# Expert stage of an attention and mixture-of-experts kernel: where TensorE transposes the gated values

## The reference, cut to what matters

```python
x = x + xattn(layernorm(x), ctx)          # two softmax attentions, 8 heads of 64, 32 batches of 256 tokens
# then a mixture of 16 experts, 4 per token, on h = layernorm(x), 8192 tokens of 256 values:
probs = softmax(h @ gate_w.T);  topk_w, topk_idx = top_k(probs, 4);  topk_w /= sum(topk_w)
g = h @ w1[e];  u = h @ w3[e]             # 256 -> 128, for each chosen expert e
act = silu(g) * u                         # silu(g) = 0.5 g (1 + tanh(g/2))
out = sum over chosen e of topk_w[e] * (act @ w2[e])     # 128 -> 256
x = x + out
```

## Time and profile before

| What | us |
|---|---|
| Median of 3 runs | 2147.49 |
| Lowest and highest | 2143.29, 2151.18 |
| The profiled execution, own time | 2151.62 |
| Its span in the trace | 2149.9 |
| PE busy over the span | 1904.3 (89%) |
| Expert stage, first gate and up product to the last gated transposes | 1507.6 to 2017.5 |

### The profile page before, as it was taken

One profiled execution on the slowest core, in us unless ns is written; L12 is line 12 of the kernel. 1 busy time (PEld: TensorE's weight loads), 2 busy tenths in 40 slices (PEclk: granted clock), 3 DMA queues, 4 the chain that ended last, 5 costly groups with the idle time before them and its releaser, 6 DMA issues.

```text
span 2149.9 us, 51903 instructions
## 1 busy us (share of the span) xinstructions
PE 1904.3 (89%) x15782; PEld 1662.2 (77%) x15783; DVE 1388.3 (65%) x3231; ACT 1233.6 (57%) x3605; POOL 1222.7 (57%) x1688
## 2 busy tenths in 40 slices
PE   6899999999999999999999999997888988888400
PEld 5788888888888888888888888885788887888400
DVE  4567666666666766667776677768655545554398
ACT  5666666667666666666666666664444444444300
POOL 3356666656666666666666666666455555555400
PEclk9999999999999999999999999998999999999755
DMA  4331111111111111111111111117475444544399
GB/s 130 111 103 45 42 49 49 52 44 39 48 46 59 44 39 42 44 52 34 39 37 44 52 34 39 37 40 214 151 222 163 147 149 147 149 146 148 117 411 361
DMA packets 158561, 210.80 MB, mean 98 GB/s; under 512 B 24224, under 2 KB 131376, under 8 KB 158512
## 3 DMA queue, kind: packets, MB, share of 16 engines
q1 hardware_dynamic: 123696, 129.95, 19.8%
q0 software_dynamic: 26112, 71.86, 9.3%
q10 hardware_dynamic: 8704, 8.39, 1.1%
HBM read 113.02 MB, written 97.12 MB: 98 GB/s over the span
## 4 chain that ended last, share of the span: by engine, by line
PE 65%; DVE 9%; issue 7%; POOL 7%; DMA 5%; ACT 4%; another core or an unknown queue 2%; SPq 0%; ACTq 0%; POOLq 0%; DVEq 0%
PE p_pt L1366 10%; PE p_gu L1570 9%; PE p_s L1349 8%; PE p_av L1386 8%; PE p_s L1287 7%; PE p_x L1287 4%; DVE z_ahead L1254 4%; POOL x_rows L575 3%; PE p_y L1591 3%; POOL probs L583 3%; PE p_x L1417 3%; PE p_s L1297 3%; DMA x_rows<-routed,slot_i 2%; ACT probs L708 2%
## 5 line engine op out<-in xcount | busy, mean ns | idle before, releaser
L583 POOL TENSOR_TENSOR probs<-probs,inv 128x256 f32<-128x256 f32 x1024 | 596.9, 613 | 410.2 <-DVE inv L971 408.9
L708 ACT ACTIVATE probs<-p_s,nmx 128x256 f32<-128x256 f32 x1024 | 473.6, 481 | 74.4 <-PE p_pt L1366 43.4
L964 DVE TENSOR_REDUCE nmx<-p_s 128x4 f32<-128x1024 f32 x256 | 312.2, 1220 | 120.2 <-PE p_s L1349 120.2
L575 POOL DMA_INDIRECT x_rows<-routed,slot_i x248 | 247.4, 998 | 134.8 <-DVE target L956 70.5
L1366 PE MATMUL p_pt<-ident,probs 128*128 128x128 f32 x2048 | 292.8, 279 | 6.8 <-POOL probs L583 4.5
L1386 PE MATMUL p_av<-probsT,val 128*64 128x256 f32 x2048 | 259.2, 389 | 9.9 <-DVE probsT L859 7.0
L1366 PEld LDWEIGHTS p_pt<-ident,probs 128*128 128x128 f32 x2048 | 230.6, 142 | 40.1 <-issue 11.7
L696 ACT COPY probsT<-p_pt 128x512 f32<-128x512 f32 x256 | 151.3, 591 | 169.1 <-PE p_pt L1366 168.3
L859 DVE COPY probsT<-p_pt 128x512 f32<-128x512 f32 x256 | 176.0, 687 | 70.6 <-PE p_pt L1366 35.7
L708 ACT ACTIVATION_READ_ACCUMULATOR probs<-p_s,nmx 128x1 f32 x1024 | 216.4, 211 | 0.0
L1211 DVE TENSOR_TENSOR xgT_lo<-p_xt,xgT_hi 128x512 fp32r<-128x512 f32 x144 | 99.1, 688 | 176.8 <-ACT xgT_hi L816 151.0
(11 more groups left out here) (234 smaller groups left out, 5206.9 us busy)
## 6 DMA issues: line engine op xcount, KB each, us to landing
y_in<-y_rows SPq DMA_DIRECT2D x32, 1024.0 KB, 8.3
xg<-x_rows SPq DMA_DIRECT2D x72, 257.0 KB
xg_more<-x_rows SPq DMA_DIRECT2D x72, 257.0 KB
rows<-in_ctx_dram SPq DMA_DIRECT2D x32, 256.0 KB, 2.7
x_in<-in_x_dram SPq DMA_DIRECT2D x32, 256.0 KB, 2.9
mid_rows<-x_mid SPq DMA_DIRECT2D x32, 256.0 KB
x_rows<-bias SPq DMA_DIRECT2D x32, 256.0 KB, 3.4
z_ahead<-mid_rows SPq DMA_DIRECT2D x24, 256.0 KB
```

The lines of the kernel that those rows point to most:

```text
L575: pool.indirect_dma_start(x_rows, bass.IndirectOffsetOnAxis(ap=slot_i[:, t, k:k + 1], axis=0), to_send[:, t, k, :], None).then_inc(last_se ...
L583: pool.tensor_tensor(pr[:, h, t, :], pr[:, h, t, :], rc[:, g:g + 1].to_broadcast([P, S]), ALU.mult).then_inc(normed_p, 1)
L708: act.activation(probs[u % 2][:, h, t, :], p_s[:, 2 * (u % 2) + h, t * S:(t + 1) * S], ACT.Exp, bias=nmx[u % 2][:, g:g + 1], accum_out=sum ...
L964: dve.tensor_reduce(nmx[i][:, :], p_s[:, 2 * i:2 * i + 2, :].rearrange("p h (t k) -> p (h t) k", t=ST), AX.X, ALU.max, negate=True).then_i ...
```

## The change

Within PE's step the gated transposes of group j-2 move from behind the gate and up products of group j to ahead of them. Their waits, semaphores and the table's transposes move with them. Nothing is added or removed, and no other engine's code changes.

```diff
                             mm = pe.transpose(p_xt[:, i, n, k, :], xg[(r + 2) % LOADS][:, n, k * P:(k + 1) * P], ident[:, :])
                     mm.then_inc(xg_t, 1)
+                if exists(j - 2):
+                    pe.wait_ge(act_set, j - 1)
+                    wait(pe, actT_lo, j - 3)
+                    if isinstance(j, int) and j in (TABLE_AT, TABLE_AT + 1):
+                        v = j - TABLE_AT
+                        pe.wait_ge(plan_step, PLAN)
+                        for c in range(TC):
+                            pe.transpose(p_at[0:1, i, (2 + c) * P:(3 + c) * P], table[:, v, c:c + 1], ident[:, :])
+                    for n in range(2):
+                        mm = pe.transpose(p_at[:, i, n * P:(n + 1) * P], gated[i][:, n, :], ident[:, :])
+                    mm.then_inc(act_t, 1)
                 if exists(j):
                     experts[r] = expert_of(j)
                     pe.wait_ge(xgT_lo, j + 1)
...
                     mm.then_inc(gu_done, 1)
-                if exists(j - 2):
-                    pe.wait_ge(act_set, j - 1)
-                    wait(pe, actT_lo, j - 3)
-                    if isinstance(j, int) and j in (TABLE_AT, TABLE_AT + 1):
...
-                    for n in range(2):
-                        mm = pe.transpose(p_at[:, i, n * P:(n + 1) * P], gated[i][:, n, :], ident[:, :])
-                    mm.then_inc(act_t, 1)
                 if exists(j - 4):
```

## The result

| What | us |
|---|---|
| Changed kernel, median of 16 runs (lowest, highest) | 2156.45 (2151.03, 2161.28) |
| Kernel before, beside it, median of 16 runs (lowest, highest) | 2146.83 (2143.29, 2151.41) |
| Ratio, 95% interval | 1.0041, 1.0034 to 1.0049 |
| The profiled execution of the changed kernel, own time, span | 2156.23, 2154.5 |

The change costs 9 us: it lies in the range and within 0.5%, but by another mechanism than the likeliest one. It was the rival "the runs get shorter". That the time still fell close to the forecast of 2150 is in part luck: the price of a shorter run happens to be small. All ratios in this document leave out one slow run, the one of `p7_after` (the last of the experiments) at 2797.94 us with a mean granted clock of 0.678 (0.96 in the others; the median in its row counts it).

What follows compares the result with a forecast made beforehand. Bound: POOL's runs of scatters and their releases, not PE's work. Steady part 0, start +1, end +1 gave +2 us: 2153.6 for the profiled execution, 2149.5 as median, say 2150; range 2134 to 2182.

Steps and rivals of the forecast that it cites:

- the runs get shorter: Rival: the fifth scatter misses its run, runs hold four, 1.805 us a scatter; +13 us, 2160; chance 0.14.
- The bound: Expert stage: POOL's runs of scatters and each release, when ACT sees PE's posts late, set the pace, not PE's work.
- Work 0: PE's step: the same two gated transposes, 0.22 us, are made elsewhere, so PE's sum changes by 0.
- The wait at the release of the down products: Gate and up products now wait for actT_lo there: start some 1.15 us late, step ends 0.9 us late.
- The wait at the other release: Where DVE's gated step releases the products: 0.55 to 0.7 us late, 0.22 of it coming back.
- The slow stretch says that 0.8 us is absorbed: Stretch from 1663.95 at low PE clock took 8.91 us against 8.93, so PE's lateness costs 0 in the steady part.
- the first rival: Rival that PE's lateness is not absorbed, a release slipping if the fifth scatter waits for y_out; +28 us, chance 0.19.
- Not absorbed: Rival: PE's lateness after the release of the down products makes releases slip; +28 us, 2176; chance 0.19.
- the circle gets faster: Rival: act_t comes 1.4 us earlier, saving ACT's tanh waits, or runs of six form; -13 us, 2136; chance 0.20.
- The start: Step 5 now waits for the plan before its products, up to 2.0 us late; taken as +1 us.
- The end: Step 142: products wait for actT_lo and start 2.6 us late; between 0 and +2.6, taken as +1 us.
- The clock: Rival: longer waits lower PE's clock twice a cycle and PE becomes the bound; +20 us, 2170; chance 0.04.

Runs made afterwards that it cites:

- p7_after: The changed kernel with POOL's second scatter of a group waiting for xgT_hi of six groups on instead of seven; 2040.71 us, 1.0012 to the kernel before.
- e1_again: The changed kernel with the expert's number read ahead of the gated transposes' waits, on a chip with late releases; 2151.23 us, 1.0016 to the kernel before.
- after_again: The changed kernel unchanged, measured once more beside the kernel before on a chip with late releases; 2157.00 us, ratio 1.0043.
- p7_before: The kernel before with POOL's second scatter waiting for xgT_hi of six groups on, not seven; 2037.19 us, ratio 1.0002.
- e4: The kernel before with 8 of the 12 gate and up matmuls, third pass left out; 1996.04 us, ratio 0.9810.

## Why the prediction was right and wrong, step by step

**The bound, right.** Not PE's work but the runs of scatters set the pace in the result: PE was busy 12 us less after and the stage still took longer. The distances of a run's parts hold too: 2.13 us from its last scatter to ACT (2.26 said) and 1.34 us to the next run.

**Work 0, right.** PE's busy time did not grow.

**The wait at the release of the down products, mis-sized.** Said: transposes 0.25 us behind actT_lo, products 1.15 us late. Measured: actT_lo ended 1661.87, transposes at 1662.02, products 1.99 us after the release against 1602.1 - 1600.79 = 1.31 said, so 1.8 late. The missing 0.6 to 0.7 is the expert's number. I had priced it at the other release only; it stands behind the transposes' wait at both. The down products behind them ended 2.75 us into the run at 1662.66, where 1.8 to 2.0 was said, and this post is the one that was held in 20 of the runs of four.

**The wait at the other release, mis-sized.** Said 0.55 to 0.7 us late, with the number's 0.6 us beginning as soon as the wait ends. Measured: the transposes start 1.23 us into the run (1.34 said, right), and the number is begun at 1823.6, after them. It takes 0.8 us to its check, with a load of 519 ns where the earlier trace rows has 298, and 0.25 to the products. They start 2.45 us into the run, against 1594.48 - 1593.47 = 1.01 before: 1.44 late, twice what was said.

**"The slow stretch says that 0.8 us is absorbed", the step that failed.** Its lateness was real and did cost nothing: the products of that run ended 1667.45, 3.50 us in, against 2.69 in the run at 1593.47 (the prediction gives the 0.8 without these rows), and the cast behind them still started at once.

```profile
1667.04 0.41 PE L1570 MATMUL p_gu<-wgu_hi,xgT_lo 128*128 x1
1667.55 0.59 ACT L816 CAST xgT_hi<-p_xt 128x512 fp32r<-128x512 f32 x1 [1.77 <-issue]
```

I read from it a room in time and carried it to another order of posts. In that run, as in the one at 1593.47, the products' post was the second in its run. In the changed kernel the gated transposes' post stands ahead of it by the change itself, and the down products' post often as well. And it was a room for one post, the gate and up products'; for the down products nothing had been measured. The change also used more than the room: 1.44 us late where up to 0.7 was said, and 1.8 where 1.15 was said. So two things failed, the sizes and the use of the room. The runs that tell them apart are e1_again's: their gate and up products are 0.46 us late (1813.18 is 1.47 into the run), less than the 0.8 that was absorbed, and still it has 25 runs of four.

**The rival "the runs get shorter", right in kind, too dear.** It said 7.22 / 4 = 1.805 us a scatter and +13. The runs of four come at 7.16, 1.789 a scatter, and ten runs of five remain; the steady part measures +6 by the scatters from 1550 to 2010 us, and the total +9. The trigger that I named under the first rival, y_out of the fifth scatter, ended 20 of the 52 runs of four; xgT_hi of seven groups on, which I had not weighed, ended 32. "2.0 is before 3.2", which spoke against it, did not hold: the down products ended 2.75 us in, and were held all the same.

**"Not absorbed" (+28), wrong.** The releases don't slip one by one; a missed fifth scatter moves into the next run, which is a loss of 0.02 us a scatter and not of 1 us a run.

**The rival "the circle gets faster", wrong.** ACT's tanh no longer waits for the transposes' post, and no time came back, so that wait was not on the path. Only one run of six stands in the changed kernel's timeline.

**The start, right in place and unresolved in price.** The plan's last step ended 1525.19 and the products of group 5 started 1526.21, 1.02 us behind it; 0.74 or 1.14 was said (the terms named, 0.25 + 0.44 + 0.6, add up to 1.29; the 1528.3 is 0.15 too early by them). Before, they started 0.86 us ahead of its end. **The end, likewise**: in step 142 actT_lo ended at 2015.00 and the products started at 2016.03, 1.03 behind; 0.45 was said. What of this reached the end is in no trace alone. On the chips without late releases the whole change costs about 2 us by p7_after, both ends included.

**The clock, wrong.** The granted clock from 1550 to 2010 us was 1.00 (2.4 GHz) in the changed kernel (0.99 in after_again) and 0.98 before, with the transposes together and more waiting. The rule of the Trainium skill (TensorE: Matmul & The Clock Gate, Part 4: PE-mode transpose), by which it should come down more often, did not show.

**What stays open.** Of the 0.43%, the number's place explains 0.27%. The other 0.16% is the wait for actT_lo, the transposes' post ahead of the products', or both; the kernels that would divide it met chips where there is nothing to divide. Which of PE's posts are held in a run is open: their place among the others orders the gate and up products and fails for the down products. Why one chip has late releases and others don't, nothing here says.

## What to carry to other kernels

When two engines are coupled by a semaphore that arrives late, ask for each post that a move delays when it now falls, who needs it, and what is read or loaded behind the moved wait; a margin in microseconds taken from one post in the old order does not carry over to another post or another order. If PE's waits are moved ahead of its large products, move the register loads ahead of the waits with them: that alone gave back 0.27% of 0.43% here. Find out what a wait is for from the code's counts and not only from the row's name: the row of the scatter at 1670.10 names a cast that it does not wait for. And compare a small change on more than one chip before calling it a property of the kernel: here the change costs 0.4% on one and about 0.1% on another.

## What the runs showed of the hardware that was not expected

- The same kernel takes 2147 us in the result and in one further set on one chip, and 2035 to 2038 us on three other chips. That the chip is the cause is not shown. The products of the expert stage take 505.0 us from first to last in the one trace (1507.6 to 2012.6) and 403.3 in that of p7_before (1500.0 to 1903.3), 102 of the 113 us between the spans. With late releases, some semaphores that PE posts during a run of scatters are seen by ACT only about 2.0 to 2.3 us after the run's last scatter has started; on the other chips POOL scatters up to 238 times in 300 us (e4), and in the trace of p7_before, from 1550 to 1850 us, ACT goes on within 0.37 us of the post in all of its 107 waits over 0.1 us.
- With late releases, gate and up products whose post is the first or second of PE in a run are seen in 0.04 to 0.92 us (kernel before), the fourth or fifth after 3.1 to 5.4. Down products that are the second post were held too (after the change: median 3.05 us).
- Reading the expert's number takes PE's sequencer 0.6 to 0.8 us from the start of the load to its check, with a load of 298 to 519 ns in the rows shown, and the products start 0.25 us later. Read ahead of the wait, none of it shows (e1_again: products 0.24 us behind the transposes, 1812.94 to 1813.18).
